# Gate statistics in one round, later ring loads and two earlier projections in a four-batch kernel

## The reference

```python
# block 1: a selective scan over ctx (512 x 256), gated by the normalised x
h  = einsum('bld,ed->bel', ctx, in_proj_w)            # input projection, 512 channels
u  = silu(causal_conv4(h) + conv_b)
dt, Bm, Cm = split(einsum('bdl,ed->bel', u, x_proj_w))
dt = softplus(dt_proj(dt) + dt_proj_b)
state = state * exp(dt * A) + dt * u * Bm             # 16 states, along 512 steps
y  = (sum over states of state * Cm + D * u) * silu(layernorm(x))   # both 512 x 512
x  = x + tanh(g0) * y.T
x  = x + tanh(g2) * ffn_ternary_weights(layernorm(x)) # 8 bit rows, gelu, w1, w2
# block 2: attention maps from ctx alone, then a float32 ffn with gelu
x  = x + tanh(g1) * (layernorm(x) @ softmax(q k^T))
x  = x + tanh(g3) * ffn(layernorm(x))
```

## Time and profile before

| | us |
|---|---|
| median of 3 runs | 968.98 |
| profiled execution | 970.21 |
| its span | 968.2 |
| PE busy | 826.2 (85%) |
| DVE busy | 762.2 (79%) |
| ACT busy | 650.9 (67%) |
| POOL busy | 518.5 (54%) |

### The profile page before, as it was taken

One profiled execution on the slowest core, in us unless ns is written; L12 is line 12 of the kernel. 1 busy time (PEld: TensorE's weight loads), 2 busy tenths in 40 slices (PEclk: granted clock), 3 DMA queues, 4 the chain that ended last, 5 costly groups with the idle time before them and its releaser, 6 DMA issues. The chain is left out here.

```text
span 968.2 us, 9285 instructions
## 1 busy us (share of the span) xinstructions
PE 826.2 (85%) x2791; PEld 407.0 (42%) x2791; DVE 762.2 (79%) x895; ACT 650.9 (67%) x970; POOL 518.5 (54%) x456
## 2 busy tenths in 40 slices
PE   8421355899799999998899999997999999898999
PEld 3110113454344444444443444443444444447887
DVE  4899897875899998957899998948899998753333
ACT  5899877673699863673799862754799863623442
POOL 0898685013998892015999881016998871022000
PEclk9755558999899999989899999989899999998999
DMA  8279962001499962301599961301699961201231
GB/s 300 55 145 245 284 120 44 1 1 44 88 219 234 234 138 86 109 1 44 117 223 227 238 141 55 109 1 43 142 226 213 221 145 54 88 1 44 90 106 65
DMA packets 46817, 119.54 MB, mean 123 GB/s; under 512 B 5793, under 2 KB 6945, under 8 KB 46257
## 3 DMA queue, kind: packets, MB, share of 16 engines
q0 software_dynamic: 16128, 58.73, 32.4%
q1 hardware_dynamic: 30640, 60.24, 18.4%
HBM read 56.03 MB, written 4.19 MB: 62 GB/s over the span
## 5 line engine op out<-in xcount | busy, mean ns | idle before, releaser
L1655 POOL TENSOR_TENSOR work<-du,bcast 128x1024 f32<-128x1024 f32 x128 | 353.3, 2804 | 16.4 <-DVE du L1307 15.6
L1273 DVE TENSOR_TENSOR_SCAN pair<-pair,work 128x512 f32<-128x512 f32 x256 | 299.3, 1215 | 28.5 <-ACT pair L891 22.3
L891 ACT ACTIVATE pair<-dt,a_neg 128x512 f32<-128x512 f32 x256 | 165.8, 682 | 18.5 <-DVE work L1280 15.5
L661 PE MATMUL bank<-stage,ring 128*128 128x512 f32 x384 | 172.9, 593 | 1.4 <-ACT stage L1129 1.4
L1280 DVE TENSOR_TENSOR work<-pair,ccast 128x1024 f32<-128x1024 f32 x128 | 156.8, 1225 | 11.6 <-ACT ccast L876 0.2
L1670 POOL DMA_DIRECT2D u<-work x112 | 125.1, 1117 | 36.7 <-DVE work L1280 15.4
L445 PE MATMUL bank<-xd,pick 128*128 128x512 bf16 x128 | 56.1, 438 | 89.0 <-ACT bcast L876 62.0
L1641 POOL TENSOR_SCALAR fst<-fst 128x1 f32<-128x1 f32 x32 | 9.2, 289 | 207.9 <-DVE fst L1500 207.7
L661 PEld LDWEIGHTS bank<-stage,ring 128*128 128x128 f32 x384 | 71.9, 190 | 80.4 <-issue 70.9
L675 PE MATMUL bank<-ring,stage 128*128 128x512 f32 x192 | 85.6, 594 | 1.7 <-ACT hx L1154 1.7
L445 PEld LDWEIGHTS bank<-xd,pick 128*128 128x128 bf16 x128 | 12.9, 101 | 141.5 <-ACT bcast L876 89.5
(11 more groups left out here) (171 smaller groups left out, 1502.1 us busy)
## 6 DMA issues: line engine op xcount, KB each, us to landing
u<-work POOLq DMA_DIRECT2D x112, 512.0 KB, 5.9
ring<-ffn_dram SPq DMA_DIRECT2D x120, 256.0 KB, 4.5
ring<-ffn_dram SPq DMA_DIRECT2D x16, 512.0 KB, 3.3
xres<-x_dram SPq DMA_DIRECT2D x4, 1024.0 KB, 5.9
stage<-w_dram SPq DMA_DIRECT2D x1, 4096.0 KB, 17.2
stage<-w_dram SPq DMA_DIRECT2D x4, 1024.0 KB, 8.7
out_dram<-stage SPq DMA_DIRECT2D x16, 256.0 KB, 2.1
ctxT<-ctxT_dram SPq DMA_DIRECT2D x4, 512.0 KB, 7.3
```

Source lines behind the costliest of these rows:

```text
L661: last = pe.matmul(banks[2 + f % 2][:], piece(b, f)[:, k * P:(k + 1) * P], xnT[:, k, :], start=k == 0, stop=k == J - 1)
L891: act.activation(pairs[s % DECAYBUFS][:, q, :], dt[:, p * HALF + q, :], ACT.Exp, scale=a_neg[:, p * HALF + q, n:n + 1]).then_inc(s_decay, 1)
L1273: dve.tensor_tensor_scan(pair[:, q, :], pair[:, q, :], rows[:, q, :], 0.0, ALU.mult, ALU.add).then_inc(s_scan, 1)
L1655: pool.tensor_tensor(work[:, s % SCANBUFS, :, :], du[:, p * HALF:(p + 1) * HALF, :], bcast[:, n % 2, :].unsqueeze(1).broadcast_to([P, HALF ...
```

## The change

Three things are done. `mixer_last` waits for all four blocks and works their statistics as four columns, three POOL instructions instead of twelve, in every batch. SP waits, ahead of the first `run`, until both last sums of the first batch are done; so the first eight ring pieces are loaded behind the first scan. And the projections j = 0 and 1 of batch 1, with their copies, move from `between` into the first turning, ahead of the gate transposes on PE and ahead of the first q copy on ACT. They go to banks 2 and 3, and j = 2 and 3 of batch 1 to banks 0 and 1, so the waits for `s_x1` and `s_qT` move to those; the first h transpose, which uses banks 2 and 3, waits for the copies. Behind the gate transposes 12 more filler matmuls go to bank 7.

```diff
@@ -65,6 +65,13 @@
 ATT_BANKS = (4, 6, 7, 6)
 MEAN_BANK = 2
 GATE_BANKS = (1, 0, 4, 5)
+
+
+def project_bank(b, j):
+
+    return (j + 2) % 4 if b == 1 else j % 2
+
+
 DT_BANKS = (0, 1, 5, 6)
 
 FFN_UP = {(5 + f // 4, f % 4): f for f in range(FT)}
@@ -331,7 +338,7 @@
         dve_m = Tally(sem("dve_m"), 4 * T)
         dve_f = Tally(sem("dve_f"), 5 * T)
         pool_s = Tally(sem("pool_s"), 0)
-        pool_m = Tally(sem("pool_m"), 2 * J + T)
+        pool_m = Tally(sem("pool_m"), 2 + T)
         pool_f = Tally(sem("pool_f"), 3 * T)
         dve_w = Tally(sem("dve_w"), 0)
 
@@ -425,6 +432,7 @@
 
             sp.sem_inc(s_stored, 1)
             load_context(1)
+            sp.wait_ge(s_last, HALF)
             for i in range(0, B - 2):
                 run(i, True, True)
             run(B - 2, True, False)
@@ -461,14 +469,14 @@
 
                 if j == 0:
                     pe.wait_ge(s_ctx, b * 16 + 16)
-                    if prev is not None:
-                        pe.wait_ge(s_x1, prev * T + T)
-                elif j == 1 and prev is not None:
+                if prev is not None and j == (2 if b == 1 else 0):
+                    pe.wait_ge(s_x1, prev * T + T)
+                elif prev is not None and j == (3 if b == 1 else 1):
                     pe.wait_ge(s_qT, prev * T + T)
                 elif j >= 2:
                     pe.wait_ge(s_inprojc, b * J + j - 1)
                 for k in range(KC):
-                    last = pe.matmul(banks[j % 2][:], ipw[:, k, j * P:(j + 1) * P], ctxT[:, k, :],
+                    last = pe.matmul(banks[project_bank(b, j)][:], ipw[:, k, j * P:(j + 1) * P], ctxT[:, k, :],
                                      start=k == 0, stop=k == KC - 1)
                 last.then_inc(s_inproj, 1)
 
@@ -561,7 +569,10 @@
                 keep_awake(24)
                 keep_awake(16)
                 pe.wait_ge(s_wq, 4)
+                project(m + 1, m, 0)
+                project(m + 1, m, 1)
                 gate_transposes(m, (0, 1, 2, 3))
+                keep_awake(12, 7)
                 q_transposes(m, (0,))
                 up1(m, 0)
                 q_transposes(m, (1,))
@@ -605,6 +616,8 @@
                     if r == 0:
                         if t:
                             pe.wait_ge(s_ev0, b * T + t)
+                        elif b == 0:
+                            pe.wait_ge(s_inprojc, J + 2)
                     elif t >= 2:
                         pe.wait_ge(s_xnTc, b * 2 * T + t - 1)
                     elif t:
@@ -741,8 +754,9 @@
 
             def between(b, m):
 
-                project(m, b, 0)
-                project(m, b, 1)
+                if m > 1:
+                    project(m, b, 0)
+                    project(m, b, 1)
                 up1(b, 2)
                 project(m, b, 2)
                 transpose_h(b, 0)
@@ -911,9 +925,9 @@
                 elif prev is not None and j == 0:
                     act.wait_ge(s_y, prev * 2 + 2)
                     act.wait_ge(s_yT, prev * T + T)
-                act.activation(xpad[:, j % 2, PAD:], banks[j % 2][:], ACT.Copy)
-
-                act.activation(u[:, j, :], banks[j % 2][:], ACT.Identity, scale=pch[:, j, TAPS - 1:TAPS],
+                act.activation(xpad[:, j % 2, PAD:], banks[project_bank(b, j)][:], ACT.Copy)
+
+                act.activation(u[:, j, :], banks[project_bank(b, j)][:], ACT.Identity, scale=pch[:, j, TAPS - 1:TAPS],
                                bias=pch[:, j, PC_CONVB:PC_CONVB + 1]).then_inc(s_inprojc, 1)
 
             def silu_u(b):
@@ -998,8 +1012,9 @@
 
             def between(b, m):
 
-                project_copy(m, b, 0)
-                project_copy(m, b, 1)
+                if m > 1:
+                    project_copy(m, b, 0)
+                    project_copy(m, b, 1)
                 gelu1(b, 2)
                 project_copy(m, b, 2)
                 h_copy(b, 0)
@@ -1131,6 +1146,9 @@
 
             def turning(m):
 
+                if m == 0:
+                    project_copy(m + 1, m, 0)
+                    project_copy(m + 1, m, 1)
                 q_copy(m, (0,))
                 gelu1(m, 0)
                 q_copy(m, (1,))
@@ -1680,16 +1698,13 @@
 
             def mixer_last(b, slot):
                 if slot == ZSTAT_SLOT:
-                    for j in range(J):
-                        st = zst[:, j, :]
-                        pool.wait_ge(s_zst, b * J + j + 1)
-                        carry_wait(pool, "pool")
-                        pool_m.link(pool, b, pool.tensor_scalar(st[:, 8:9], st[:, 2:3], 1.0 / D, LN_EPS,
-                                                                ALU.mult, ALU.add))
-                        pool_m.link(pool, b, pool.tensor_tensor(st[:, 9:10], st[:, 8:9], expo[:, 0:1], ALU.pow))
-                        carry_wait(pool, "pool")
-                        pool.tensor_scalar(st[:, 10:11], st[:, 1:2], st[:, 9:10], 1.0, ALU.mult,
-                                           ALU.mult).then_inc(s_zrs, 1)
+                    pool.wait_ge(s_zst, b * J + J)
+                    carry_wait(pool, "pool")
+                    pool_m.link(pool, b, pool.tensor_scalar(zst[:, :, 8], zst[:, :, 2], 1.0 / D, LN_EPS,
+                                                            ALU.mult, ALU.add))
+                    pool_m.link(pool, b, pool.tensor_tensor(zst[:, :, 9], zst[:, :, 8], expo[:, 0:1].broadcast_to([P, J]), ALU.pow))
+                    carry_wait(pool, "pool")
+                    pool.tensor_tensor(zst[:, :, 10], zst[:, :, 1], zst[:, :, 9], ALU.mult).then_inc(s_zrs, J)
 
             def turning(b):
                 for t in range(T):
```

## The result

The changed kernel took 961.13 us (median of six runs, 956.54 to 964.68) against 969.57: a ratio of 0.9919, 95% interval 0.9897 to 0.9940, or 7.9 us less (here and below a gain is worked out from the ratio, not from the two medians). The forecast was 961.2. In a second set of runs it was 961.0 against 968.73, ratio 0.9929 (0.9906 to 0.9952).

What follows compares the result with a forecast made beforehand. DVE's first-scan waits for POOL were taken as the time to win, with a chain of full engines behind; 4.1 + 0.5 + 1.3 + 1.9 = 7.8 us off 968.98 gave 961.2 us, range 958 to 966.

Steps and rivals of the forecast that it cites:

- the clock term: First turning: PE's clock taken as held through the rest, so sixteen matmuls take 3.62 us instead of 4.93; 1.3 us (0 to 1.3).
- the first rival: First turning: PE's clock is lost, so the gain comes without 1.3 us; 962.5 us, chance 0.25.
- The bottleneck: First scan: DVE waits 6.0 us for POOL, held by its accumulating transfers and gate statistics; later scans gain nothing.
- The statistics' round: POOL's gate statistics: one round of 1.6 us replaces four taking 5.7 us, giving POOL back 4.1 us (0 to 4.3).
- What is late next: Ahead of the gate transposes: PE's fillers and projections, not DVE, come last; transposes start at 157.6 instead of 161.69, 4.1 us.
- Overlap of the two scan edits: First scan: statistics and ring loads overlap, together worth at most 6.0 us of DVE's waits plus about 0.4.
- 0.5 us of quicker transposes: First turning: the first gate transposes run quicker once PE reaches them without a stop, so the first sum begins 0.5 us sooner.
- Projections: Stage behind the first turning: 3.65 us of PE work leaves, DVE's quantisation limits; first down product 1.9 us sooner (0 to 3.65).
- The sum: Whole kernel: 4.1 + 0.5 + 1.3 + 1.9 = 7.8 us less, 961.2 us for the median; forecast chance 0.45.
- the first term: Start of the gate transposes in the first turning: 4.1 us earlier, with ACT coming forward by 2.6 us.
- signs of being right: Included no DVE wait for POOL past 110 us, gate transposes near 157.6, q transpose near 165.5, down product near 186.5.
- signs of being wrong: ACT's probabilities still at 147, q transposes over 8.5 us behind, clock below 1.00 before 200 us, DVE idle before second quantisation.

## Why the prediction was right

The number and most of the steps held; the clock term did not. What took place in the turning is the first rival, the clock lost, to which I had given 0.25 and 962.5 us.

**The bottleneck.** That POOL's lateness counts only in the first scan, with the ring loads and the statistics as its two causes, held: the waits went, all but 0.4 us, and in the second scan there is no wait for POOL, as before. The statistics' round costs 2.1 us, not 1.6.

**What is late next.** Right, and the best-placed step: PE's fillers and projections end at 157.0 (157.6 forecast), DVE's product at 154.6 (155.6). The term was 4.7 us instead of 4.1, for two reasons read from the trace: ACT came forward by 2.8 us instead of 2.6, and the projections and the gate transposes each start 0.2 us before the modelled end of what is ahead of them. Taking 16 fillers away moved the transposes to DVE's product, as this step demands.

**Overlap of the two scan edits.** Wrong in the size: I had them share most of the stall, and they add (3.2 and 3.4 give 6.6 at the gate transposes). The step that was off is that without the loads POOL's lead would cover most of the old statistics: with the loads moved alone, 2.85 of the 3.71 us stay. The total was safe from this, since it went by PE's queue and not by DVE's waits.

**Clock term.** This step failed. The 0.5 us of quicker transposes came (5.2 at the q transposes); of the 1.3 us only 0.1 did (6.07 to 5.99 us from the first to the second q transposes), since the clock fell at 165.5 us; I had called it near even and taken it as held. One of the two rows it was weighed by was misread: in the kernel before the clock fell at 160.4, 3.85 us after the stop at 156.55 and not 4.2, and the other fall came after 3.3. The rule of the Trainium skill that speaks against the change, "TensorE: Matmul & The Clock Gate", section "Part 4: PE-mode transpose", goes with what was seen: the q transposes at 164.92 did not stop the fall, though 0.4 us of any work might not have. With the ring loads moved alone the clock fell at 159.3, within the gate transposes, 1.1 us after they had begun and 3.8 after the fillers ended, which goes with it too; no run here tests the rule by itself. The 1.3 us would not have come in full in any case: with 28 fillers and the clock held that stretch takes 5.35, 0.7 less than before, DVE's sums being next.

**Projections.** 1.9 us forecast, 2.1 measured: the second h transposes wait for DVE's quantisation (1.48 us idle in PE's timeline), and 5.2 us of lead become 7.3. Against that stand the 2 us by which they put off the gate transposes, so beside both scan edits, by the traces, the projections are worth next to nothing. The first down product is at 187.3 against 188.7, but 1.2 of these 1.4 us lie between the first and second q transposes (5.99 against 7.22) and are clock. The sum was right to count both, and a reader should not take the third edit for a source of the gain.

**The sum.** 7.3 us are found in the first trace and 7.0 in the second where 7.8 were forecast: in the first +0.6 in the first term, +0.2 in the projections and -1.2 in the clock. The median moved by 7.9, with an interval of 5.8 to 10.0. That the number agrees to 0.1 us is luck: one term was missed, two others came out larger, and the falls of the clock alone move a run of these kernels by more than that.

**The signs.** Of the signs of being right, the gate transposes (157.01), the first q transposes (164.92) and the second scan (9.0 us earlier, 1.7 of it the fall missing in the first pass) came. The down product was 0.8 later than 186.5, the statistics took just over 2 us, and one wait for POOL of 0.4 us was left past 110. Of the signs of being wrong one came: a clock below 1.00 ahead of 200 us.

## What to carry to other kernels

Ask of each engine on the way to a join what it has queued ahead of it, fillers included: here they were what came last as soon as the data was early. An experiment whose stretch improves and whose total does not should be read stage by stage; two of these hid 0.5 and 1.2 us of gain behind a fall of the clock elsewhere. One trace of each kernel is not enough to say what a filler does to the clock, since the same kernel loses more or less at the same place. And a full PE can still be a slow one: the row of the granted clock, not the busy share, pointed to the step sizes, whose split was worth 7 us in the median and 5.0 by the trace, against 7 to 8 for the whole change.

## What was not expected of the hardware

- A row of four f32 products with 16 rows of weights behind 1 us of transposes lets the granted clock fall to 1.2 GHz though PE never stands still (in the kernel before; the other traces have at most 0.34 us of idle time there). It costs up to 1.2 us in the products themselves and up to 2.9 in the sixteen matmuls behind (6.47 against 3.62 us). It came in 27 of 33 such places (eleven traces, three passes). With two in a row it did not fall in any of nine (three traces). Which of the small number of rows, the f32 type and the transposes ahead it takes, no run separates.
- The fall comes in some executions and not in others at the same place. The start of the tail takes 8.5 to 8.6 us in six of the fourteen traces and 5.7 to 5.8 in eight. In the first turning the changed kernel's sixteen up products ran between 4.5 and 6.5 us with the same twelve fillers.
- In the nine traces in which the clock fell in the rest of the first turning, it did so 2.1 to 4.0 us after PE had stopped.
- POOL's power takes 0.55 us for one column and 1.04 for four, so it is not all fixed cost, while the scaling of one column takes 0.19 and of four 0.20.
